# A decoder layer on one core: the state-space scan by half batches, four channel chunks in a step

## The reference

```python
# 1: state-space scan (16 states), residual on x; layernorm first
dt = softplus(x_proj[:16] @ dt_proj + b);  dA = exp(dt*A);  dBx = dt*B*x
h = dA_t*h + dBx_t                 # over the 128 tokens, for each sequence, feature, state
y = sum_n h*C + D*x
x = x + y
# 2: cross attention on a second layernorm, 32 heads of 128, keys and values from ctx
q, k, v = rms(ln(x)) @ w_q.T, ctx @ w_k.T, ctx @ w_v.T
x = x + ln(x) + softmax(mask(q @ k.T + bias)) @ v @ w_out.T
# 3: a linear layer with a low-rank mixture, on a third layernorm
x = x + ln(x) @ (W + sum_e p_e B_e A_e).T + b
```

## Time and profile before

| | |
|---|---|
| median of 3 | 993.44 us |
| profiled execution | 994.63 us, its span 992.5 us, mean granted TensorE clock 0.974 |
| busy: PE, DVE, ACT, POOL | 938.2, 645.1, 486.3, 474.4 us |
| scan (first `dbx` to last `times_c`) | 81.78 to 406.56 us |
| first query product of attention | 444.73 us |

### The profile page before, as it was taken

The page is one execution under the profiler, slowest core; times in us unless marked ns, Lnnn a source line. Parts: engine busy times, 40 slices in busy tenths (PEclk is TensorE's granted clock), DMA queues, the critical chain, the costliest instruction groups (busy, mean ns, idle before and its releaser), DMA issues.

```text
span 992.5 us, 14723 instructions
## 1 busy us (share of the span) xinstructions
PE 938.2 (95%) x4648; PEld 772.2 (78%) x4648; DVE 645.1 (65%) x819; ACT 486.3 (49%) x1058; POOL 474.4 (48%) x291
## 2 busy tenths in 40 slices
PE   8996899989898989988999999999999999999998
PEld 7665677767686767766888888888888888888867
DVE  5289889999999999752454454544545444444675
ACT  4485354546354545243455545454454554545631
POOL 2112566666666666403445444554445544455422
PEclk9977999999899999999999999999999999999999
DMA  8345655655455543215744454444444444444302
GB/s 287 112 132 159 219 169 177 196 177 180 159 185 195 170 162 133 106 47 159 265 140 142 141 149 152 135 148 137 158 143 135 144 139 151 149 135 148 104 19 85
DMA packets 92315, 149.95 MB, mean 151 GB/s; under 512 B 10192, under 2 KB 34896, under 8 KB 92160
## 3 DMA queue, kind: packets, MB, share of 16 engines
q1 hardware_dynamic: 87888, 132.72, 41.7%
q10 hardware_dynamic: 4400, 16.91, 5.5%
HBM read 113.81 MB, written 35.78 MB: 151 GB/s over the span
## 4 chain that ended last, share of the span: by engine, by line
PE 61%; DVE 27%; DMA 4%; ACT 3%; issue 3%; POOL 1%; SPq 0%; DVEq 0%; ACTq 0%; POOLq 0%
DVE misc L972 11%; PE acc L378 9%; PE acc L380 8%; PE acc L379 8%; PE misc L378 6%; PE misc L380 6%; PE misc L379 6%; PE misc L580 6%; DVE w L982 6%; DVE misc L966 6%; PE misc L606 6%; PE misc L572 3%; DMA k_scratch<-kst 2%; DMA wraw<-in_wk 1%; DMA base<-in_ctxT 1%
## 5 line engine op out<-in xcount | busy, mean ns | idle before, releaser
L1136 POOL TENSOR_TENSOR y<-y,w 128x1024 f32<-128x1024 f32 x64 | 153.5, 2398 | 144.8 <-DVE w L982 144.8
L1152 POOL TENSOR_TENSOR wq_lo<-wq_raw,wq_hi 128x512 fp32r<-128x512 f32 x64 | 83.2, 1300 | 289.4 <-ACT wq_hi L801 289.4
L1063 DVE TENSOR_TENSOR ot_lo<-misc,ot_hi 128x512 fp32r<-128x512 f32 x64 | 44.3, 692 | 172.3 <-ACT ot_hi L844 172.3
L972 DVE TENSOR_TENSOR_SCAN misc<-dA,misc 128x1024 f32<-128x1024 f32 x64 | 146.9, 2296 | 10.1 <-ACT dA L666 3.3
L837 ACT ACTIVATE prob<-prob,negm 128x128 f32<-128x128 f32 x256 | 99.8, 391 | 79.4 <-DVE negm L1047 79.4
L378 PE MATMUL acc<-wv_hi,ctx_hi 128*128 128x512 f32 x256 | 108.0, 422 | 29.9 <-ACT vst L660 17.6
L378 PE MATMUL misc<-z_hi,wq_hi 128*128 128x512 f32 x256 | 106.6, 417 | 5.4 <-POOL wq_lo L1152 5.4
L826 ACT ACTIVATE q_sb<-misc 128x512 f32<-128x512 f32 x64 | 38.2, 597 | 142.9 <-PE misc L380 142.9
L378 PE MATMUL acc<-wo_hi,ot_hi 128*128 128x512 f32 x256 | 106.8, 417 | 0.0
L379 PE MATMUL acc<-wv_lo,ctx_hi 128*128 128x512 f32 x256 | 105.5, 412 | 0.0
L380 PE MATMUL acc<-wv_hi,ctx_lo 128*128 128x512 f32 x256 | 104.5, 408 | 0.0
(11 more groups left out here) (142 smaller groups left out, 1941.2 us busy)
## 6 DMA issues: line engine op xcount, KB each, us to landing
k_scratch<-kst SPq DMA_DIRECT2D x64, 256.0 KB, 2.7
bc<-xp_scratch ACTq DMA_DIRECT2D x16, 1024.0 KB, 5.9
v_scratch<-vst SPq DMA_DIRECT2D x32, 512.0 KB, 4.0
wq_raw<-in_wq SPq DMA_DIRECT2D x64, 256.0 KB, 3.3
k_sb<-k_scratch SPq DMA_DIRECT2D x64, 256.0 KB, 2.6
v_sb<-v_scratch SPq DMA_DIRECT2D x64, 256.0 KB, 2.6
wo_raw<-in_wo SPq DMA_DIRECT2D x64, 256.0 KB, 2.9
wraw<-in_wk SPq DMA_DIRECT2D x32, 256.0 KB, 4.0
```

Source lines behind the costliest of these rows:

```text
L972: dve.tensor_tensor_scan(h_ps, dA[c % 2][:, :, :].rearrange("p b s -> p (b s)"), h_ps, 0.0, ALU.mult, ALU.add).then_inc(da_free, 1)
L1136: pool.tensor_tensor(y[:, c], y[:, c], w[:, c], ALU.add).then_inc(y_ready, 1)
L1152: pool.tensor_tensor(wq_lo[p][:], wq_raw[p][:], wq_hi[p][:].bitcast(F32), ALU.subtract).then_inc(wq_lo_done, 1)
```

## The change

The scan goes through sequences 0 to 3 with all 16 states, then 4 to 7: `NSTEP` = 32 steps of 128 x 2048 (four channel chunks x 512). B is broadcast over the chunks within the DVE instruction; the working tile takes all four banks of `misc`, so y, x, dt of the second half, and z go through the two `acc` banks as further slots in the sequence of sums (`slot`). Only the first half of x goes through layernorm, projection and softplus before the scan; the second half's follow among the sums and scan steps. The first half's residual, layernorm and z are made between scan steps 21 and 29. Attention starts with 4 value sums left. The second half's z is made in head steps 5 to 8. The FFN weights load at head step 30 (before: steps 2 and 3).

```diff
-NSTEP = N * C
+NSTEP = 2 * N
+def slot(g, j):
+    more = 0
+    if g >= 1:
+        more += HB if g == 1 and j < HB else HB + 1 if g == 1 and j < KP else HB + 1 + C
+    if g >= 5:
+        more += HB
+    if g >= 7 or g == 6 and j >= KP:
+        more += C
+    return SUMS * g + j + more
...
+            def dA_exp(k, c):
+                half, n = k // N, k % N
+                if n == 0 and c == 0:
+                    act.wait_ge(sp_done, half + 1)
+                act.wait_ge(da_free, k + 1)
+                act.activation(dA[k % 2][:, c, :, 1:S], dt_[:, half, c, :, 1:S],
                                ACT.Exp, scale=negA[:, c, n:n + 1]).then_inc(da_ready, 1)
...
-                return min(NSTEP, max(0, LEAD + PER * s // SPAN))
+                return min(C * NSTEP, EARLY + 10 * s // 9)
...
+            def times_c(k):
+                dve.wait_ge(bc_in[k % TRI], 16 * (k // TRI + 1))
+                if k >= 2:
+                    dve.wait_ge(y_ready, k - 1)
+                dve.wait_ge(da_free, k + 3)
+                dve.tensor_tensor(cols(w[:, k % 2]), misc[:, :, :], every(bc[k % TRI][:, 1]), ALU.mult).then_inc(prod_done, 1)
...
+            for k in range(NSTEP):
+                dbx(k)
+                scan_step(k)
+                times_c(k)
+                if k == 9:
+                    softplus_rest(1, flat(u[:, 1]))
+                if k == 12:
+                    softplus_sum(1)
+                if k == 13:
+                    times_x(1)
+                if k == 21:
+                    x1_sum(0)
+                if k == 22:
+                    x1_moments(0)
+                if k == 24:
+                    z_norm(0)
+                if k == 25:
+                    new_base(0)
...
             for m in range(3, 2 * NG):
-                for j in range(added, LEAD + PER * (m - 3) // 2):
-                    add_y(j)
-                added = LEAD + PER * (m - 3) // 2
+                upto = 1 + 29 * (m - 3) // 12
+                for k in range(added, upto):
+                    add_y(k)
+                added = upto
                 low_w(m, wv_hi if m % 2 else wk_hi, wv_lo if m % 2 else wk_lo)
```

More of the change, by code:

```diff
@@ L106, in decoder_layer @@
[L106 to L116, removed]
@@ L119, in decoder_layer @@
-        with ExitStack() as scan:
[L120 to L125, removed]
+        var = sb(whole, "var", [P, 2, B])
+        rstd = sb(whole, "rstd", [P, 2, B])
+        tmp8 = sb(whole, "tmp8", [P, 2, B])
+        with ExitStack() as first:
+            xpw = sb(first, "xpw", [P, C, RX])
+            dtw = sb(first, "dtw", [R, D])
+            maskraw = sb(first, "maskraw", [P, B, S], U8)
+            rest = sb(first, "rest", [P, C, HT])
@@ new lines, in decoder_layer @@
+        with ExitStack() as heads:
+            wq_raw = [sb(heads, f"wq_raw{i}", [P, C, P]) for i in pair]
+            wq_hi = [sb(heads, f"wq_hi{i}", [P, C, P], F32R) for i in pair]
+            wq_lo = [sb(heads, f"wq_lo{i}", [P, C, P], F32R) for i in pair]
+        sb(whole, "early_end", [P, 6, C * P])
+        with ExitStack() as scan:
+            dt_ = sb(scan, "dt_", [P, 2, C, HB, S])
+            u = sb(scan, "u", [P, 2, C, HB, S])
+            w = sb(scan, "w", [P, 2, C, HB, S])
+            dA = [sb(scan, f"dA{i}", [P, C, HB, S]) for i in pair]
+            bc = [sb(scan, f"bc{i}", [P, 2, HT]) for i in range(TRI)]
+            y = sb(scan, "y", [P, B, C, S])
@@ new lines, in dt_proj @@
+            def dt_proj(half, c, out):
+                return pe.matmul(out, dtw[:, c * P:(c + 1) * P], xp_sb[0:R, half], start=True, stop=True)
+            k_sum(0, 4)
+            for b in range(HB):
+                x_transpose(b, misc[:, b]).then_inc(xt_ps, 1)
+            k_sum(0, 5)
+            pe.wait_ge(params_in, 16 * 7)
+            pe.wait_ge(xt_evac, HB)
+            x_proj(0, misc[:, 0]).then_inc(xp_ps, 1)
+            k_sum(0, 6)
+            pe.wait_ge(xp_evac, 1)
+            for c in range(C):
+                dt_proj(0, c, misc[:, c]).then_inc(dt_ps, 1)
@@ L540, in f_input @@
             def f_input(half, *free):
-                bank = acc if half else misc
                 for c in range(C):
                     pe.wait_ge(*free[c])
+                    out = misc[:, c] if half else four[c]
                     for b in range(HB):
@@ new lines, in _ @@
+            xp_store(0)
+            inverse_root(2, 0, of_half(1))
+            k_copy(0, 6)
+            for k in range(2):
+                load_bc(k)
+            for c in range(C):
+                act.wait_ge(sp_max, c + 1)
+                act.activation(w[:, 0, c], misc[:, c], ACT.Abs, bias=dtb[:, c:c + 1]).then_inc(sp_abs, 1)
+            act.wait_ge(sp_abs, C)
+            act.activation(w[:, 0], w[:, 0], ACT.Exp, scale=-1.0).then_inc(sp_exp, 1)
+            k_copy(0, 7)
+            act.wait_ge(sp_exp, 1)
@@ new lines, in z_norm, with new_base @@
+            def z_norm(half):
+                refine(3 + half, both, of_half(half))
+                for b in range(half * HB, (half + 1) * HB):
+                    norm(y_tok[:, b], base[:, b], b, 1).then_inc(zn_done, 1)
+            def new_base(half):
+                part = of_half(half)
+                dve.wait_ge(zn_done, (half + 1) * HB)
+                link(dve.tensor_tensor(tmp8[:, 0, part], mv[:, part, 0], rstd[:, 0, part], ALU.mult))
+                link(dve.tensor_scalar(tmp8[:, 1, part], rstd[:, 0, part], 1.0, None, ALU.add))
+                for b in range(half * HB, (half + 1) * HB):
+                    last = dve.tensor_scalar(base[:, b], base[:, b], tmp8[:, 1, b:b + 1], tmp8[:, 0, b:b + 1], ALU.mult,
+                                             ALU.subtract)
+                link(last)
```

889 lines of the change are left out of this document (462 added, 427 removed).

## The result

| | before | changed |
|---|---|---|
| median | 992.85 us (991.77 to 994.21, 4 runs) | 1028.73 us (1027.78 to 1031.77, 4 runs) |
| ratio, 95 % interval | | 1.0352 (1.0329 to 1.0374) |
| profiled execution, its span | 994.63, 992.5 us | 1031.77, 1030.0 us |
| end of the last `times_c` | 406.56 us | 433.67 us |
| first query product | 444.73 us | 454.56 us |

The account below looks back on a forecast made before the run. The scan was taken to set the pace before attention, PE's products to bound attention. Step 29's end at 378.8, hand-over to 424.0, then attention and 2.1 outside the span gave 979.6, stated as 979 us; range 956 to 1000.

Parts of the forecast that it names:

- first scan ends: End of the first scan step: first product at 61 plus 2.3 and 4.5, so 67.9 us.
- 29 steps without waits: Scan steps of 2048 columns at 9.27 us each: 268.8 us for 29.
- moved work and its turns: DVE pieces moved between scan steps: 21.1 us, plus 16 us for taking turns with POOL.
- POOL's order: POOL's queue: additions to y behind `low_w` make DVE wait, 5 us in all; bounds 0 and eleven times 4.6.
- late decays and B's copy: ACT's queue early in the scan: the prediction's sum had no such wait, 0 us.
- hand-over: From the end of scan step 29 to the first query product: decay, copies, 15 sums and weight split, 45.2 us.
- first query to the end of the span: Attention onward: 547.8 us as before, 9.7 added for value sums and transposes, 4 gone.
- Start: Start of the scan: first product at 61 us, 21 us earlier than before; bounds 56 and 67.
- width: Length of a scan step: 2048 columns cost 9.27 us, 23 us gone over the scan; bounds 9.98 and 9.1.
- the slow rival: POOL's queue: `low_w` ahead of `add_y` stops DVE at all eleven places, 50.6 us, total 1025; chance 0.10.
- Turns: Moved DVE pieces wait for POOL's 4.6 us additions: three and a half waits, 16 us; range 0 to 37.
- 25 us in my weighing: Exclusive port pair catches tiny DVE operations too: turns nearer 25 than 16 us; the rival built on it had 0.13.

Follow-up runs that it names:

- pool_one_more: The changed kernel with one more addition to y in GpSimd's queue ahead of each weight split; 1018.95 us.
- lead_alone: The changed kernel with only the decays' order altered: three more ahead up to slot 50, then given out more slowly; 1049.15 us.
- early_decays: The changed kernel with up to 3 more decays ahead of the first eight slots' copies on ScalarE; 1029.62 us.
- lead_kept: later_gates with the lead of three decays kept up to slot 50, then taken back faster; 968.58 us, ratio to before 0.9739.
- three_no_inside: all_four without the edit of the pieces, which stand behind the product by C again; 999.75 us.
- pieces_inside: The changed kernel with VectorE's eight inserted pieces put between the scan and the product by C of their step; 1027.55 us.
- all_four: The changed kernel with entry_first, pool_one_more, pieces_inside and early_decays together; 990.8 us, ratio to before 0.9966.
- entry_first: The changed kernel with the second half's layernorm moved from the head steps to behind the scan; 1008.3 us, ratio to before 1.0144.
- two_orders: lead_alone plus one more addition ahead of each split on GpSimd and the earlier transfer of B and C; 1009.4 us.
- later_gates: all_four plus earlier B and C transfer, decays after slot 50 given out more slowly, y turned behind three last value sums; 980.55 us.

## Why the prediction was wrong, step by step

The sum against the profiled execution, 979.6 against 1031.8 (the slowest of the four, 3 us above their median):

| term | forecast | measured |
|---|---|---|
| first scan ends | 67.9 | 67.66 |
| 29 steps without waits (measured: what is left) | 268.8 | 268.7 |
| moved work and its turns | 37.1 | 44.1 |
| POOL's order, to step 29 | 5 | 16.8 |
| late decays and B's copy | 0 | 10.2 |
| step 29 ends | 378.8 | 407.4 |
| hand-over | 45.2 | 47.2 |
| first query to the end of the span | 553.5 | 575.4 |
| outside the span | 2.1 | 1.8 |

- **Start, width, hand-over: right.** The addition ahead of the start met the second `low_w` as forecast: it took 6.59 us and ended at 58.40, forecast 58.5. The forecast of the step from two rows of another width, 9.27 us, was 0.06 to 0.09 low. That a broadcast operand costs nothing was an open bound and is now measured.
- **POOL's order: the mechanism right, its count wrong.** I worked out 14.1 us from the end of a scan to the product behind a `low_w`; the place at 398 us took 14.6. At the two places that I counted DVE waited 4.63 us (step 7, priced at 4.9) and 3.57 (step 24), 8.2 against the 5 in my sum, and the others I called covered by a step of slack. Four of those came too, with 13.8 us: steps 5, 12, 19 and 29. That makes six places with 22.0 us in all in the scan, 16.8 before step 29 ends. By the number of places, five or more, the slow rival applied, at less than half of its 50.6 us; that its 1025 is near the measured time is luck, since most of the miss lies in other terms. The slack was there only if `low_w` came on time, and it comes by ACT's queue (POOL waited 180.4 us for the splits), which comes by DVE's (56.7 us). I priced one turn of a ring as a line. pool_one_more shows the term (13 us at step 29), lead_alone that it can grow as the decays stand further ahead (50.8 us).
- **ACT's queue: a term left out.** I never checked in it whether the decays of steps 2 to 4 are there in time. They are not: the transfer of B and C, 14 waits with 21.8 us, eight slots of turned x and dt, and copies stand between. It is worth 10.2 us in the trace, but by early_decays nothing as long as POOL's order stops DVE a little later; with POOL's order mended lead_kept gains 12 us by it.
- **Turns: sized too low.** 16 us forecast, 23 measured (18.3 to 20.7 in the three other kernels that are alike up to there). The Trainium skill (SBUF — State Buffer, SBUF: two separate sides) says that the port pair shared by DVE and GpSimd is held for a whole instruction, by which the operations of a few columns are caught too. The rows above agree with it: 4.47 us for eight columns. That gave 25 us in my weighing; I took the lower value because no row showed it. What I missed is that the turns depend on POOL's lateness and on the pieces' place together: the pieces take 44.9 and 45.7 us behind the product with POOL in time (three_no_inside, pool_one_more), 41.5 ahead of it with POOL late (pieces_inside), and 33.7 with both mended (all_four), where their durations alone are 21.1.
- **Entry of the attention: the largest single miss, 21.9 us.** I counted two value sums and 32 transposes on PE, and gave the second half's layernorm no cost on DVE and ACT, though it was moved work like the rest: its pieces stand in DVE's queue between a head's scores and its probabilities, while the pipeline is still being filled and has no slack, and PE's products behind the two longer waits ran at the 1.2 GHz level. entry_first shows 20.4 us. The wait of the second query product in the earlier trace rows, 2.54 us, was a hint that the entry is tight.
- **The chances.** Four terms were wrong in the same direction, and three of them hang together in one ring; I had treated them as independent, and gave 0.17 to slower.
- **What I left out in reading the kernel before.** I put PE's waits for the copies down to decays that wait for the scan (18.7 us). ACT's copies of keys also waited 46.6 us for the stores of earlier ones there, which I did not look at; in the changed kernel that is 7.2 us. No term of the sum hangs on it.

What stays open: where exactly the 8 us of two_orders come from, which of the two edits of later_gates gains what, and how the 21.4 us of the entry, of which the root accounts for 4.0 and the width for 5.8, divide for the rest between order and clock.

## What to carry to other kernels

Where two engines' queues are interleaved by formulas (here `due` on ACT, `upto` on POOL), walk the ring before pricing a term: for each instruction that frees something, list what stands ahead of it in its queue and what that waits for, and see if it comes back to the same engine. An order that is a little late then costs again and again (here at six of eleven places), and an edit of one engine's order alone can be worth nothing or be a loss (early_decays, lead_alone), while the edits of all orders, with norm and pieces moved, together gave 60 us. Work that is moved into the filling of a pipeline is priced on every engine it touches; put it where those engines are known to be idle.

## What the runs showed of the hardware

- A DVE product with an operand that is broadcast over four chunks of 512 columns from PSUM or SBUF takes 2.29 to 2.30 us for 2048 columns, and a plain one 2.29 (`times_x` at 58.43): no cost of the broadcast. The scan takes 4.43 us for 2048 columns.
- A DVE operation of eight columns, 0.17 us alone, took 2.43 and 4.47 us beside GpSimd additions of 4.68, each ending within 0.03 us of an addition's end, if the three additions of the row are of equal length. DVE's products with an operand in PSUM kept 2.29 us beside the same additions.
- A decay of 508 columns takes 711 ns and one of 1016 took 1139: with half the width ACT is busy 89.1 us with the decays of the scan in place of 72.8.
